# Rows scattered into expert slots while a sentence is routed, and experts' tiles loaded as contiguous rows

## The chip, the cores and the metric

The kernel runs on one core of a Trainium2 chip, in float32. The metric is the device time of one execution in microseconds (us); the time before is the median of three executions. Beside them stands one profiled execution with its trace, and every row shown below is from it. Engines: PE is TensorE, DVE is VectorE, ACT is ScalarE, POOL is GpSimd, SP is SyncE, which here only issues transfers.

## What is computed

```python
x = x + attention_a(layernorm(x))    # 8 sentences x 512 tokens x 256, 16 heads of 64, distance slopes, causal
x = x + experts(layernorm(x))
x = x + attention_b(layernorm(x))    # 8 heads of 128, rotary positions, causal
x = x + experts(layernorm(x))

def experts(x):                      # the same weights both times
    h = x * rsqrt(mean(x * x) + eps) * norm_w
    logits = h @ gate_w.T + gate_b
    vals, idx = top_k(logits, 2); wts = softmax(vals)          # 2 of 8 experts
    t1 = h @ mlp1_w[e].T + mlp1_b    # 256 -> 512
    act = min(glu, 7) * sigmoid(1.702 * glu) * (clip(lin, -7, 7) + 1)
    y = act @ mlp2_w[e].T + mlp2_b   # 256 -> 256
    return sum over the two chosen experts of y * wts
```

## The kernel before

Four stages follow each other: attention_a (0 to about 905 us), experts(0) (to 1186), attention_b (to about 1900), experts(1) (to 2195), and a tail that ends at 2215.5. Each engine has one instruction stream written out by hand, executed in order; engines meet through semaphores.

**Attention.** A unit u is a pair of heads; `bt, p = divmod(u, 8)` gives sentence bt (0 to 7) and unit p in it. A unit of attention_a takes 13.9 us, one of attention_b 11.4. In attention_a the POOL scales the probabilities of two heads per unit (`scale`, L1178) and adds some small normalising steps; in attention_b it does the rotary sums (L2058, L2069) and once a sentence a residual of 1024 columns (L2039).

**Routing.** Sentence bt-1 is routed during sentence bt. Its normalised rows are in the SBUF tile `hh`, one for all sentences; SP stores them to the DRAM tensor `hD` (`store`, 512 KB for each sentence and layer). The gate's top two give for each token two slots, a slot being expert * 4096 + rank among that expert's tokens. DVE writes them into `dI` (`route`, piece 4, L298; in attention_a in unit 6 of the sentence). POOL then scatters token numbers to those slots (`put_ids`, L311, an indirect DMA of 128 times 4 bytes to `slotD`, 8 for each sentence). As `dI` is one tile, L298 waits until the id scatters of the sentence before have landed (`d_sc`). SP fetches the id lists back (`fetch_ids`, L337), PE picks the used parts (`pick`), and DVE works out for each tile of 128 rows a column of `idx` (rows to gather) and of `place` (rows of the output) in six pieces (`places`).

**Experts.** Each experts stage has 71 tiles of 128 rows: 40 from the first six sentences, 31 from the rest. For a tile, POOL gathers 128 rows of 1 KB out of `hD` by `idx` (`gather`, L329); PE transposes them (L2286), multiplies up (L2301 to L2303), transposes the activation (L2312), multiplies down (L2325, L2327); ACT and DVE copy and activate between (ACT L2385, L2391, L2399, L2405, DVE L2473 to L2490); POOL scatters the 128 result rows to `yD` by `place` (`scatter`, L2600). Gathers run seven tiles ahead. The ids of the last two sentences are put inside the stage: eight before tile 0, mixed with the first gathers, and eight in tiles 16 to 27. The stream of POOL in the stage:

```python
for a in range(NS):
    if a + 7 < NS:
        gather(e, ph, q, a + 7)
    if 16 <= a < 28 and a % 3 != 0:
        put_ids(e, ph, BL, (a - 16) - (a - 16 + 1) // 3)
    ...
    scatter(a)
```

The functions that the change touches:

Of the kernel before, what the change touches and what calls it, by code (L numbers as in the profile page):

```python
# [59 lines left out]
def program(nc, T):  # L60
# [8 lines left out]
    with ctx:  # L69
# [4 lines left out]
        hD = [dram(f"hD{i}", [NT * 128, D]) for i in range(2)]  # L74
# [9 lines left out]
        hDv = [h.rearrange("(b p t) d -> b p t d", p=128, t=TT) for h in hD]  # L84
# [20 lines left out]
        idx = sb("idx", [128, NSP], I32)  # L105
        place = sb("place", [128, NSP], I32)
        etab = sb("etab", [1, NSP], I32)
# [23 lines left out]
        ls = sb("ls", [128, 2, L1])  # L131
        pl = sb("pl", [128, 2, L1])
# [140 lines left out]
        def route(e, q, ph, bt, piece, if8=None):  # L273
# [20 lines left out]
            else:  # L294
                e.wait_ge(r_op, 2 * s + 2)
                if s:
                    e.wait_ge(d_sc, 128 * s)
                e.scalar_tensor_tensor(dI[:], if8[:, :, 0:2], float(NT * 128), dF[:], ALU.mult, ALU.add).then_inc(r_sl, 1)  # L298
# [16 lines left out]

        Gs = []

        def gather(e, ph, q, a):
            if a == 0:
                e.wait_ge(r_ls, 4 * ph + 2)  # L320
                e.wait_ge(q.d_h, 16 * K1)
                e.wait_ge(q.p_xs, NB - 2)
            if a == L1:
                e.wait_ge(r_ls, 4 * ph + 4)
                e.wait_ge(q.d_h, 16 * NB)
# [27 lines left out]
        def listing(e, ph, k, piece):  # L353
# [61 lines left out]
            elif piece == 11:  # L415
                e.wait_ge(r_tab, b + 10 + k)
                if ph or k:
                    e.wait_ge(r_val, 2 * ph + k)
                e.tensor_scalar(Sel[:, 0, 0:n], ra[:, 0:n], cst[:, C_P:C_P + 1], None, ALU.is_equal)
# [30 lines left out]
        def places(e, ph, k, piece):  # L450
            n, off, b = (L1, L2)[k], (0, L1)[k], 4 * (2 * ph + k)
            v, w = ls[:, 0, 0:n], ls[:, 1, 0:n]
# [3 lines left out]
            elif piece == 1:  # L456
                e.wait_ge(r_st, b + 1)
                e.tensor_scalar(pl[:, 0, 0:n], v, float(NT * 128), float(NT * 128), ALU.is_gt, ALU.mult).then_inc(r_st, 1)
            elif piece == 2:
                e.scalar_tensor_tensor(pl[:, 1, 0:n], v, 0.0, cst[:, C_PAD + off:C_PAD + off + n], ALU.is_equal,  # L460
                                       ALU.mult).then_inc(r_st, 1)
            elif piece == 3:
                e.tensor_scalar(w, v, -1.0, 0.0, ALU.add, ALU.max).then_inc(r_st, 1)
            elif piece == 4:
                e.wait_ge(r_st, b + 4)
# [2376 lines left out]
```

## Time and profile before

| what | value |
|---|---|
| median of three executions | 2229.8 us (2229.5 to 2231.53) |
| profiled execution | 2217.43 us, span 2215.5 |
| PE busy | 2052.4 us, 93% |
| DVE, ACT busy | 1568.7 (71%), 1442.5 (65%) |
| POOL busy | 1308.6 (59%), 1466 instructions |
| mean granted PE clock | 0.98 |

A busy share counts time in which an engine has an instruction in work. "Idle before" is the time an engine sat before an instruction, with what released it; a releaser "remote" or "another core or an unknown queue" is one that the records of this core do not name, and "issue" is time in which no recorded thing was waited for.

### The profile page before, as it was taken

The page shows a single profiled execution, that of the slowest core. Times are in us where ns is not written, and L with a number is a line of the kernel's source. Part 1 is how long each engine was busy: PE and PEld are TensorE (multiplying, and loading weights), DVE is VectorE, ACT ScalarE, POOL GpSimd, SP SyncE. Part 2 cuts the span into 40 slices and gives each one's busy share as a digit, 9 for nine tenths or more (in the row PEclk, how much of TensorE's full clock was granted, in tenths as well). Part 3 has the DMA queues.
Part 4 walks back from the last instruction along what each step waited for, and adds up shares of the span by engine and source line. Part 5 has one row for each costly group of instructions (what it writes and reads, how often), then busy time and mean ns, then how long its engine had stood idle before and what let it go on. Part 6 is the DMA issues. An engine that isn't in the chain of part 4 may idle for free.

```text
span 2215.5 us, 38087 instructions
## 1 busy us (share of the span) xinstructions
PE 2052.4 (93%) x11638; PEld 1629.8 (74%) x11638; DVE 1568.7 (71%) x4433; ACT 1442.5 (65%) x3763; POOL 1308.6 (59%) x1466
## 2 busy tenths in 40 slices
PE   7899999999999999797998999999999999888895
PEld 6677777777777776575776787887878877676774
DVE  7867676868686868465666778677786776656567
ACT  5768787878686867433444868767777676633344
POOL 4665464646464655566665556667576565556563
PEclk9999999999999999999999999999999999999998
DMA  4330020101010000523341101011010001533347
GB/s 147 133 111 30 1 30 1 30 1 30 1 30 1 20 1 22 176 94 77 103 146 58 39 30 39 12 38 46 13 39 30 1 20 58 169 84 97 98 127 246
DMA packets 59932, 134.42 MB, mean 61 GB/s; under 512 B 12948, under 2 KB 31156, under 8 KB 58840
## 3 DMA queue, kind: packets, MB, share of 16 engines
q1 hardware_dynamic: 42008, 94.68, 12.8%
q0 software_dynamic: 17728, 37.32, 6.5%
q8 instruction: 100, 1.64, 0.4%
q14 instruction: 96, 0.79, 0.2%
HBM read 83.59 MB, written 48.40 MB: 60 GB/s over the span
## 4 chain that ended last, share of the span: by engine, by line
PE 68%; DVE 13%; ACT 6%; issue 5%; another core or an unknown queue 4%; POOL 1%; DMA 1%; SPq 0%; ACTq 0%; DVEq 0%; POOLq 0%
PE bank L639 5%; PE bank L657 5%; PE bank L2327 5%; PE bank L679 5%; PE bank L1568 4%; PE bank L624 3%; PE bank L625 3%; PE bank L1553 2%; PE bank L2301 2%; PE bank L2303 2%; PE bank L2302 2%; PE bank L1469 2%; PE bank L570 2%; PE bank L572 2%
## 5 line engine op out<-in xcount | busy, mean ns | idle before, releaser
L1178 POOL TENSOR_TENSOR P<-P,rc 128x128 f32<-128x128 f32 (+3 forms) x512 | 354.4, 723 | 342.0 <-DVE rc L984 341.8
L976 DVE CUSTOM_DVE_ANT_0 P<-bank,tab 128x512 f32<-128x512 f32 (+3 forms) x512 | 241.3, 485 | 105.6 <-PE bank L625 102.2
L807 ACT ACTIVATE P<-P,mn 128x128 f32<-128x128 f32 (+3 forms) x512 | 281.7, 552 | 34.2 <-DVE mn L976 30.7
L818 ACT COPY PT<-bank 128x512 f32<-128x512 f32 (+1 forms) x384 | 194.0, 516 | 107.3 <-PE bank L639 98.1
L2058 POOL TENSOR_TENSOR rf<-rp 128x512 f32<-128x512 f32 x128 | 163.9, 1281 | 134.9 <-DVE rp L1891 134.1
L2069 POOL TENSOR_TENSOR q<-rf,q 128x512 fp32r<-128x512 f32 x128 | 163.1, 1296 | 117.5 <-ACT q L1693 117.2
L639 PE MATMUL bank<-cst,P 128*128 128x128 f32 x1280 | 207.2, 276 | 15.4 <-POOL P L1178 9.6
L2600 POOL DMA_INDIRECT yD<-Yf,place x142 | 144.5, 1018 | 123.5 <-ACT Yf L2405 90.3
L624 PE MATMUL bank<-q 128*128 128x512 f32 (+3 forms) x512 | 185.2, 373 | 21.3 <-DVE mn L976 11.6
L329 POOL DMA_INDIRECT Gf<-hD,idx x142 | 144.8, 1020 | 74.4 <-issue 37.1
L639 PEld LDWEIGHTS bank<-cst,P 128*128 128x128 f32 x1280 | 153.0, 141 | 43.0 <-POOL P L1178 12.9
L952 DVE TENSOR_TENSOR q<-bank,q 64x512 fp32r<-64x512 f32 x256 | 175.8, 687 | 7.3 <-ACT q L798 1.3
L2399 ACT COPY ATf<-bank 128x256 f32<-128x256 f32 x142 | 53.4, 376 | 176.5 <-PE bank L2312 81.3
L798 ACT CAST q<-bank 64x512 fp32r<-64x512 f32 x256 | 146.5, 572 | 11.2 <-PE bank L572 8.0
L1720 ACT ACTIVATE P<-P,rc 128x128 f32<-128x128 f32 (+3 forms) x256 | 123.1, 552 | 46.6 <-DVE rc L1906 46.6
L2327 PE MATMUL bank<-W2f,ATf 128*128 x568 | 153.2, 394 | 0.0
L657 PE MATMUL bank<-PT,V 128*64 128x512 f32 (+3 forms) x1024 | 152.0, 439 | 1.3 <-ACT PT L818 1.3
L625 PE MATMUL bank<-q 128*128 128x512 f32 (+3 forms) x512 | 152.4, 323 | 0.0
L1568 PE MATMUL bank<-PT,V 128*128 128x512 f32 (+3 forms) x512 | 151.6, 439 | 0.9 <-ACT PT L1730 0.8
L311 POOL DMA_INDIRECT slotD<-cst,dI x128 | 128.7, 1005 | 39.8 <-issue 32.1
L1710 ACT ACTIVATE P<-P,mn 128x128 f32<-128x128 f32 (+3 forms) x256 | 141.0, 555 | 0.4 <-DVE mn L1898 0.4
L1730 ACT COPY PT<-bank 128x512 f32<-128x512 f32 (+1 forms) x192 | 93.5, 517 | 72.2 <-PE bank L1553 72.0
(272 smaller groups left out, 6037.2 us busy)
## 6 DMA issues: line engine op xcount, KB each, us to landing
hD<-hh SPq DMA_DIRECT2D x16, 512.0 KB
yg<-yD SPq DMA_DIRECT2D x14, 512.0 KB, 4.6
X<-in_x SPq DMA_DIRECT2D x8, 512.0 KB, 4.6
stage<-in_w SPq DMA_DIRECT2D x8, 512.0 KB, 3.7
w1hD<-W1A SPq DMA_DIRECT2D x8, 512.0 KB
w1lD<-stage SPq DMA_DIRECT2D x8, 512.0 KB
rD<-xn SPq DMA_DIRECT2D x8, 512.0 KB
W1lf<-w1lD SPq DMA_DIRECT2D x1, 4096.0 KB
```

The costliest lines, as they stand in the source:

```text
L624: e.matmul(o, QS[:, k, hl, ts], KS[:, k, hl, 0:w], start=True, stop=False)
L625: i = e.matmul(o, QS[:, k, hl, ts], KL[:, k, hl, 0:w], start=False, stop=True)
L639: i = e.transpose(o[:, at:at + 128], P[:, h % 3, OFF[t] + cc * 128:OFF[t] + cc * 128 + 128], ident)
L657: i = e.matmul(bank[6][64 * hl:64 * hl + 64, cc * 128:512], V[:, g % 2, cc, col:col + 64], PT[:, hl, PTO[cc]:PTO[cc] + w], start=cc == 0, ...
L807: i = e.activation(ps, ps, ACT.Exp, bias=mn[:, pb, t:t + 1], scale=-1.0, accum_out=rs[:, pb, t:t + 1])
L818: e.copy(PT[:, h % 2, PTO[cs[0]]:PTO[cs[0]] + w], bank[4 + n % 2][:, 0:w]).then_inc(q.a_pt, 1)
L952: e.tensor_tensor(L, bank[j][own, :], H.bitcast(F32), ALU.subtract).then_inc(v_q, 1)
L976: e.tensor_tensor_reduce(out=P[:, pb, OFF[t]:OFF[t] + w], in0=score(h, t), in1=tab[:, 512 - w:512], scale=-SLOPES[h % 16], scalar=3e38, op ...
L1178: i = e.tensor_tensor(ps, ps, rc[:, h % 3, t:t + 1].broadcast_to([128, w]), ALU.mult)
L1568: i = e.matmul(bank[6][:, cc * 128:512], V[:, g % 2, cc, col:col + 128], PT[:, PTO[cc]:PTO[cc] + w], start=cc == 0, stop=cc == TT - 1)
L2058: e.tensor_tensor(rf[:, j], rp[:, j, 0], rp[:, j, 1], ALU.add).then_inc(p_rf, 1)
L2327: i = e.matmul(o, AT[:, k, kc], W2[:, ex, kc].rearrange("p x n -> p (x n)"), start=False, stop=kc == 1)
```

## The change

`hD` becomes `hS`, 8 * 4096 rows for each layer: a region of 4 MB for each expert. Each normalised row is written to its two slots when its sentence is routed. In parts:

- SP's 16 stores of `hh` to `hD` are gone. In their place `put_rows`: 128 POOL indirect scatters (8 for each sentence and layer) of 128 rows of 1 KB from `hh` to `hS` by `dI`. The next sentence's `hh` and `dI` wait until they landed (`q.d_h` to 128 * bt).
- SP gets `fill`, 16 transfers DRAM to DRAM, one for each sentence and layer: a rotary table of 128 times 4 KB is written to each of the 8 regions (4 MB each time), so that slots nobody takes hold finite numbers. Two for each layer at its start, the others each after the fetch of the sentence's input.
- The 142 POOL gathers are gone. SP issues 142 `load`s in their place: the start row is read from `rtab` into a register (`value_load`), and 128 consecutive rows, 128 KB, are loaded. Load a waits until tile a - 4 was transposed; loads 0 to 3 are issued before the stage. `rtab` is one small DVE instruction in the listing.
- `places` has three pieces in place of six (no `idx`).
- `put_ids` moves. Attention_a: it was two each after units 7, 0, 1 and 2; now rows stand there (units 6, 7, 0, 1) and ids follow at units 2 to 5, two each; in the last sentence four ids each at units 2 and 3. Attention_b: rows two at unit 6, three each at units 7 and 0; ids two each at units 1 to 4, in the last sentence four each at units 1 and 2. Inside experts: sentence 6's ids one each in tiles 0 to 7, its last rows before the stage, and sentence 7's eight ids and eight rows in tiles 16 to 27, four for three tiles.
- In attention_b L298 moves from step 53 to step 47 of the sentence. `pick` moves from tile 31 to 33, `places` from 32, 33 to 34 to 36. SP's other transfers of an experts stage are interleaved with the loads.

```diff
+        def put_rows(e, q, ph, bt, n, hh):
+            s = NB * ph + bt
+            t, j = divmod(n, 2)
+            if n == 0:
+                e.wait_ge(r_sl, s + 1)
+                e.wait_ge(d_z, 32 + 16 * (s + 1))
+            e.indirect_dma_start(hS[ph], bass.IndirectOffsetOnAxis(ap=dI[:, t, j:j + 1], axis=0), hh[:, t],
+                                 None).then_inc(q.d_h, 16)
+
+
+        def fill(e, ph, s):
+            e.wait_ge(d_z, 32 + 16 * (NB * ph + s))
+            block = hS[ph].rearrange("(k s p r) d -> s p k (r d)", k=E, s=NB, p=128)[s]
+            src = T["tab"][1][:, 1:3].rearrange("p a b -> p (a b)").rearrange("p (a n) -> p a n", a=1)
+            e.dma_start(block, src.broadcast_to([128, E, 1024])).then_inc(d_z, 16)
...
-        def gather(e, ph, q, a):
+        def load(e, ph, q, a):
             if a == 0:
-                e.wait_ge(r_ls, 4 * ph + 2)
-                e.wait_ge(q.d_h, 16 * K1)
+                e.wait_ge(r_sel, 2 * ph + 1)
+                e.wait_ge(q.d_h, 128 * K1)
...
             if a > 3:
                 e.wait_ge(f_x, NS * ph + a - 3)
-            rows = hD[ph][0:K1 * N] if a < L1 else hD[ph]
-            e.indirect_dma_start(Gs[ph][:, a % 4], None, rows, bass.IndirectOffsetOnAxis(
-                ap=idx[:, a:a + 1], axis=0)).then_inc(d_g[a % 4], 16)
+            row = e.value_load(rtab[0:1, a:a + 1], min_val=0, max_val=E * 32 - 1)
+            rows = hS[ph].rearrange("(n p) d -> p n d", p=128)[:, bass.ds(row, 1)]
+            e.dma_start(Gs[ph][:, a % 4], rows.rearrange("p n d -> p (n d)")).then_inc(d_g[a % 4], 16)
...
@@ POOL, attention_a, after each unit
-                        if p == 7 and bt and bt + 1 < NB:
-                            for n in range(4 if bt == K1 else 2):
-                                put_ids(e, 0, bt - 1, n)
-                        if bt == K1 + 1 and p == 0:
-                            for n in range(4, 8):
+                        if bt and p > 5:
+                            for n in (2 * p - 12, 2 * p - 11):
+                                put_rows(e, q, 0, bt - 1, n, hh)
+                        elif bt > 1 and p < 2:
+                            for n in (2 * p + 4, 2 * p + 5):
+                                put_rows(e, q, 0, bt - 2, n, hh)
+                        elif bt == K1 + 1 and p < 4:
+                            for n in range(4 * p - 8, 4 * p - 4):
                                 put_ids(e, 0, bt - 2, n)
-                        elif 1 < bt <= K1 and p < 3:
-                            for n in (2 * p + 2, 2 * p + 3):
+                        elif 1 < bt <= K1 and p < 6:
+                            for n in (2 * p - 4, 2 * p - 3):
                                 put_ids(e, 0, bt - 2, n)
...
@@ POOL, experts
-                        if a + 7 < NS:
-                            gather(e, ph, q, a + 7)
-                        if 16 <= a < 28 and a % 3 != 0:
-                            put_ids(e, ph, BL, (a - 16) - (a - 16 + 1) // 3)
+                        if a < 8:
+                            put(BL - 1, a)
+                        elif 16 <= a < 28:
+                            for n in range(4 * (a - 16) // 3, 4 * (a - 15) // 3):
+                                put(BL, n)
```

## Rows read from the trace of the kernel before

**Rows 1.** The page: busy time, share of the span, instructions.

```profile
PE 2052.4 (93%) x11638; PEld 1629.8 (74%) x11638; DVE 1568.7 (71%) x4433; ACT 1442.5 (65%) x3763; POOL 1308.6 (59%) x1466
```

**Rows 2.** Busy time by stage: window, length, engines, granted clock, DMA share, GB/s.

```profile
110.00:905.00 795.00, 771.93 (x4707) 599.10 (x4707) 590.50 (x1854) 602.19 (x1589) 448.59 (x612) 1.00 0.10 30
905.00:1190.00 285.00, 245.19 (x1230) 193.35 (x1225) 168.97 (x458) 112.87 (x317) 172.83 (x179) 0.96 0.35 100
...
1890.00:2195.00 305.00, 263.77 (x1356) 208.70 (x1354) 190.16 (x521) 134.60 (x380) 180.19 (x175) 0.96 0.40 121
```

**Rows 3.** Groups of POOL: busy us, mean ns, idle before and releasers.

```profile
L329 POOL DMA_INDIRECT Gf<-hD,idx x142 | 144.8, 1020 | 74.4 <-issue 37.1 <-PE bank L2286 21.6 <-DVE place L468 15.2
L2600 POOL DMA_INDIRECT yD<-Yf,place x142 | 144.5, 1018 | 123.5 <-ACT Yf L2405 90.3 <-issue 33.2
L311 POOL DMA_INDIRECT slotD<-cst,dI x128 | 128.7, 1005 | 39.8 <-issue 32.1 <-DVE dI L298 6.3 <-PE bank L1537 1.2
```

**Rows 4.** Waits in 905 to 1190: us in total, times, longest.

```profile
ACT ATf L2399 <- remote: 33.0, 10, 5.3
```

**Rows 5.** Waits in 1890 to 2216.

```profile
ACT ATf L2399 <- remote: 42.2, 12, 7.2
```

**Rows 6.** Timeline of one stall in experts(0), all engines: start, us, instruction, idle before.

```profile
1042.85 0.39 PE L2303 MATMUL bank<-W1A,XTlf 128*128 x1
...
1044.78 0.42 DVE L2479 TENSOR_SCALAR glf<-bank 128x256 f32<-128x256 f32 x1 [3.45 <-remote]
...
1046.21 0.37 ACT L2399 COPY ATf<-bank 128x256 f32<-128x256 f32 x1 [5.33 <-remote]
...
1046.72 0.41 PE L2312 MATMUL bank<-cst,acf 128*128 128x128 f32 x2 [3.49 <-ACT ATf L2399]
```

**Rows 7.** Timeline of PE, first instruction of two tiles without a stall.

```profile
1053.14 0.38 PE L2286 MATMUL bank<-cst,Gf 128*128 128x128 f32 x2
...
1055.95 0.38 PE L2286 MATMUL bank<-cst,Gf 128*128 128x128 f32 x2
```

**Rows 8.** Waits in 2172 to 2196, after the last gather of experts(1).

```profile
ACT ATf L2399 <- remote: 2.5, 1, 2.5
```

**Rows 9.** Timeline of units 5 and 6 of sentence 2, attention_a.

```profile
339.44 0.91 POOL L1154 TENSOR_TENSOR X<-X,bout 128x256 f32<-128x256 f32 x1
342.91 2.76 POOL L1178 TENSOR_TENSOR P<-P,rc 128x128 f32<-128x128 f32 x4 [2.57 <-DVE rc L984]
...
344.04 0.66 DVE L298 SCALAR_TENSOR_TENSOR dI<-if,dF 128x8 int32<-128x8 f32 x1
...
344.93 1.41 DVE L952 TENSOR_TENSOR q<-bank,q 64x512 fp32r<-64x512 f32 x2
...
346.49 0.39 PE L624 MATMUL bank<-q 128*128 128x512 f32 x1
```

**Rows 10.** Timeline: last id scatter before a fetch of the lists, and the fetch.

```profile
827.08 0.95 POOL L311 DMA_INDIRECT slotD<-cst,dI  x1 [0.30 <-issue]
...
835.79 0.37 SPq L337 DMA_DIRECT2D idT<-slotD  x1
...
2050.77 0.97 POOL L311 DMA_INDIRECT slotD<-cst,dI  x1 [0.30 <-issue]
...
2054.36 0.37 SPq L337 DMA_DIRECT2D idT<-slotD  x1
```

**Rows 11.** Timeline of SP: the transfer that the fill follows in sentence 2.

```profile
327.93 0.42 SPq L1256 DMA_DIRECT2D X<-in_x  x1
```

**Rows 12.** Window as in rows 2: the busiest stretch of DMA.

```profile
890.00:905.00 15.00, 10.45 (x74) 7.09 (x73) 11.67 (x46) 11.85 (x36) 7.70 (x12) 1.00 0.94 400
```

**Rows 13.** Timeline of attention_b: residual of one sentence; unit 4 and L298 of the next.

```profile
1436.67 2.41 POOL L2039 TENSOR_TENSOR xl<-X,xl 128x1024 f32<-128x1024 f32 x1
...
1534.62 1.28 POOL L2058 TENSOR_TENSOR rf<-rp 128x512 f32<-128x512 f32 x1 [0.88 <-DVE rp L1891]
...
1561.59 1.11 DVE L298 SCALAR_TENSOR_TENSOR dI<-if,dF 128x8 int32<-128x8 f32 x1
```

More of the change, by code:

```diff
@@ L1297, in sync @@
                             fetch_x(bt + 2)
+                        if bt and bt + 1 < NB:
+                            fill(e, 0, bt + 1)
                         if bt == 0:
@@ L1314, in sync @@
                             e.dma_start(w1lD[0:1, :, 0:512], first[1]).then_inc(d_w1o, 16)
+                            fill(e, 0, 0)
+                            fill(e, 0, 1)
+                    for a in range(4):
+                        load(e, 0, q, a)
                     e.wait_ge(d_w1o, 32 * E + 48)
@@ L2095, in gpsimd @@
                             residual(bt - 1)
-                        if u == NU - 1:
-                            for a in range(4):
-                                gather(e, 1, q, a)
                         if p == 7 and bt + 2 < NB:
@@ L2664, in sync @@
                         store_r(BL - 1)
+                        for a in range(4):
+                            load(e, ph, q, a)
                         e.wait_ge(q.a_q, 2 * NU)
@@ new lines, in sync @@
+                    for a in range(4, NS):
+                        load(e, ph, q, a)
+                        if a == 16:
+                            store_r(BL)
+                        if a == 37:
+                            fetch_ids(e, ph, 1)
+                        if not last:
+                            if a == 19:
+                                e.wait_ge(q.m_lg, 2 * NB)
+                                stage_in(0)
+                                stage_in(1)
+                            elif a % 4 == 0 and 28 <= a <= 64:
+                                stage_in((a - 20) // 4)
+                            if a == 64:
+                                begin[4](e)
+                            elif a == 65:
+                                begin[5](e)
+                        else:
+                            if a in (19, 22, 25, 28):
+                                fetch_r((a - 19) // 3)
+                            elif a in (45, 49, 53, 57):
+                                fetch_r((a - 29) // 4)
+                            if a == 65:
+                                for k in range(4):
+                                    e.wait_ge(d_y[k], 16 * ph * ((NS + 3 - k) // 4) + 16 * ((LA + 3 - k) // 4))
+                                e.wait_ge(q.h_in, NB)
+                                fetch_rows(0, 1)
+                                fetch_rows(0, 0)
+                            elif 65 < a < NS - 1:
+                                fetch_rows((a - 64) // 2, 1 - a % 2)
@@ L2765, in _ @@
             late = first[4](e)
-            second[4](e, late)
+            second[4](e, late, begin)
             late = third[4](e)
```

190 lines of the change are left out of this document (86 added, 104 removed).

## Prediction

> **What bounds the kernel now.** I read the page first: PE is busy 93% of the span, POOL 59% [rows 1]. Then the windows by stage: in attention_a PE works 771.93 us of 795 at full clock, so little is to be had there; in the first experts stage it works 245.19 of 285 us at a clock of 0.96, in the second 263.77 of 305 [rows 2]. The two stages hold 81 us in which PE idles, attention_a 23 us in 795. So the question is what the change does to PE's idle time in the experts stages, and whether what it puts into the attention stages breaks a cover there.
>
> A tile of an experts stage without a stall takes PE 1055.95 - 1053.14 = 2.81 us [rows 7]; 71 tiles would take 200 us, and the stage takes 285 with its start. What fills the gap is seen in the waits: ACT sits 33.0 us in 10 pieces before the copy of the transposed activation with a releaser the records don't name, up to 5.3 us each; in the second stage 42.2 us in 12 [rows 4, 5]. In one such stall, PE has begun the last up product at 1042.85 and is done within half a us; DVE takes the result up at 1044.78 and ACT at 1046.21, after 3.45 and 5.33 us of idle time, and PE then waits 3.49 us for ACT [rows 6]. Nobody was busy: engines are told late that PE is done. After the last gather of the second stage such waits are down to one of 2.5 us [rows 8], though the result rows are still scattered. The attention window 110 to 905 has no such row among its 25 longest waits, with its id scatters in groups of two to four. I read from this that the late signals come with dense indirect transfers of POOL, above all where gathers and scatters alternate without a gap.
>
> An indirect transfer holds POOL for 1.0 us and leaves 37.1 / 122 = 0.30 us before the next can start, 1.3 us together, whichever of the three kinds it is [rows 3]. A tile with gather and scatter costs POOL 2.6 us of PE's 2.81; one with an id scatter too costs 3.9.
>
> **The change part by part, experts.** It removes one indirect of each tile and adds no work to PE. POOL is at 1.3 us for most tiles, 2.6 in tiles 0 to 7, and 1.3 * (1 + 4/3) = 3.0 in tiles 16 to 27.
> - Late signals: 33.0 + 42.2 = 75.2 us of ACT's idle time [rows 4, 5]. PE loses less than ACT, 3.49 of 5.33 [rows 6], a factor of 0.65: 49 us. Bounds: 0 if they have nothing to do with the gathers, and 75 if PE loses all that ACT loses. I take 49: the part after the last gather [rows 8] speaks for nearly all.
> - Tiles 16 to 27: POOL's mean is (2 * 3.9 + 2.6) / 3 = 3.5 us before and 3.0 after, against PE's 2.81, so 12 * 0.5 = 6 us for each stage; about half lies under the stalls already counted, so 3 each, 6 in all (0 to 12).
> - Loads: 128 KB for each tile of 2.81 us is 47 GB/s, the DMA engines have moved 400 in a busy stretch [rows 12], and a load is issued three tiles (8.4 us) before its use. Its cover is these 8.4 us. I take 0. The wait of SP for `f_x` holds the transfers queued behind it on SP; those are input rows and weights with tiles of slack, 0 to 5 us.
> - The four gathers before the stage waited for `place`, 15.2 us [rows 3], but PE is still busy with the last output projection then. I take 0 (0 to -4, as a free POOL could bring tile 4 sooner).
> Sum for experts: -49 - 6 = -55 us, bounds +5 and -91 (75 + 12 + 4).
>
> **Attention_a, the id scatters moved later.** This is where I see a new wait. Before, the ids of sentence bt-2 were put by unit 2. Now their last pair stands after unit 5: POOL ends L1154 at 339.44 + 0.91 = 340.35, so the second scatter starts at about 341.8 [rows 9]. L298 of the next sentence comes on DVE at 344.04 [rows 9], and waits for them to land. How long a landing takes is bounded by the fetches of the lists, which wait for it: 2054.36 - 2050.77 = 3.6 us and 835.79 - 827.08 = 8.7 us, both with the fetch's own issue in them [rows 10]. Landing is thus at 345.4 to 350.5; I take a little over the middle, 348.3 (6.5 us), as this is an attention stage, like the 8.7. DVE stands 4.3 us. Queued behind L298 are the maxima of the next scores and at 344.93 the rotation of q, 1.41 us, for which PE's scores at 346.49 wait with 346.49 - 346.34 = 0.15 us of slack [rows 9]. PE loses about 4 us in each of sentences 2 to 6: +20 us. Bounds: 1.4 - 0.15 = 1.2 and 6.3 a sentence, +6 to +32.
> The fill bears on this. It starts right after the fetch at 327.93 [rows 11] and moves 4 MB. At 400 GB/s [rows 12] that is 10.5 us, over by 339, before the ids. At half that speed it is 21 us and lies across them.
> The Trainium skill, "DMA: Bandwidth & Descriptors", section "Latency and other measured facts", says that copies between HBM tensors whose rows lie 4 MiB apart ran at about half the rate of closer or padded rows (103 against 214 GB/s). The fill writes pieces 4 MB apart; by that figure a fill would last about 40 us. No row of before has such a transfer.
>
> **Attention_a, POOL.** The 64 row scatters come on top of the ids, and each pair of either costs 2.6 us. POOL works 448.59 of 795 us [rows 2] and otherwise waits for DVE before a scale; that idle time is the cover. After unit 5, where it has L1154 to do as well, 2.57 us are left before the next scale against a pair's 2.6 [rows 9]; if such a cover is gone, PE's transposes of the scaled probabilities are late by what is missing. Only the groups of four of the last sentence don't fit (5.2 us). +3 us (0 to 6).
>
> **Attention_b, POOL.** Here POOL is tighter: rotary sums follow the residual L2039, 2.41 us [rows 13], without a pause. The id pair now put behind it pushes PE's scores; half of 2.6 us is caught by later slack, 1.25 * 5 sentences = 6, and +3 for the groups of four in the last sentence: +9 (0 to 20). L298 is moved six steps of 11.4 / 7 = 1.6 us earlier, from 1561.59 to about 1552; the ids after unit 4 are issued behind the rotary sum of 1534.62, so by 1538.5 [rows 13], and with 8.7 us to land they are 5 us early: 0. Stores of `hh` removed, DVE pieces removed: off the path, 0.
>
> **Sum.** 2217.4 - 55 + 20 + 3 + 9 = 2194 for a profiled execution, 23 us less. The runs shown have a median 12 us over the profiled one; I carry the difference: 2229.8 - 23 = 2207.
>
> **Rivals.**
> 1. *The late signals stay.* They are not tied to gathers; an SP load or any dense traffic also brings them. For it: in the experts stages much besides the gathers is going on, and the DMA share is 0.35 to 0.40 against 0.10 [rows 2]. Against: rows 8, where traffic goes on. Then only the 6 us of tiles 16 to 27 and some 4 more remain: -10 + 32 = +22, 2252. This is the case on the other side: it decides once less than 26 us of the 49 go.
> 2. *The fill holds the ids.* At 21 to 40 us a fill lies across the ids put at 340 to 343; if their landing is 9 us later, PE loses 45 us more in the five sentences: -23 + 45 = +22, again 2252; at 4 us later, 2227.
> The Trainium skill, same page, section "Queues, rings and completion order", says that a completion's semaphore write comes after all earlier writes of that DMA engine, across its queues. By this rule the ids of a busy fill are signalled only with the fill's issued pieces; no row here shows it.
> 3. *Landing is quick* (3.6 us), PE loses more than 0.65 of ACT's idle time, and attention_b takes less: -62 + 6 + 3 + 5 = -48, 2182.
>
> **How the numbers follow.** Forecast 0.52 (own range 2192 to 2222); rival 1 0.2; rival 2 0.16, of which a third ends near 2227 and the rest slower; rival 3 0.12. Within 0.2%, about 4.5 us and what this kernel's measurement can tell, lies 0.07 in all. Faster: 0.50 + 0.12 + 0.01 = 0.63. Slower: 0.30. The range goes from 2182 to 2252.
>
> **What would show it.** Right: the rows with the unnamed releaser in both experts stages fall under 10 us, tiles follow at about 2.9 us, each stage is some 27 us shorter; in attention_a a wait of DVE for L298 on the ids, 4 us in each of five sentences, and that stage 20 us longer; attention_b 9 us longer. Wrong: stages of 285 us with the same ACT waits (rival 1), or waits of DVE over 8 us in sentences 2 to 6 with DMA busy (rival 2), or PE waiting for a load.

## The result, and the profile after

The changed kernel takes 2277.65 us (median of four executions, 2273.32 to 2281.53), the kernel before beside it 2230.06 (2229.5 to 2231.53). The ratio is 1.0212, with a 95% interval of 1.0192 to 1.0232: 2.1% slower. The profiled execution has a span of 2279.7 us against 2215.5, so 64.2 us more; the medians differ by 47.6, because the profiled execution of before lies 12 us under its median and that of after 4 us over its own. What follows explains the 64.2. The page of the changed kernel, where [rows 1] stood before:

```profile
span 2279.7 us, 38939 instructions
...
PE 2068.0 (91%) x11638; PEld 1647.5 (72%) x11638; DVE 1585.4 (70%) x4425; ACT 1443.7 (63%) x3763; POOL 1293.3 (57%) x1452
...
PEclk9999998989899999999999999999999999989998
```

POOL is a little less busy, PE works the same instructions. (PEclk is the granted clock of PE in 40 equal slices, in tenths of full speed.) A cut by stage shows where the time went. A stage is read here from the first and last transposition of the experts' tiles, which are the group L2286 before and L2301 after (first and last start are the last numbers of a row). Before, experts(0) and then experts(1):

```profile
L2286 PE MATMUL bank<-cst,Gf x142: 272/273/421, 913.7 to 1173.0; 128*128 128x128 f32 x142
...
L2286 PE MATMUL bank<-cst,Gf x142: 272/273/421, 1931.5 to 2183.2; 128*128 128x128 f32 x142
```

After:

```profile
L2301 PE MATMUL bank<-cst,Gf x142: 270/273/421, 993.0 to 1229.6; 128*128 128x128 f32 x142
...
L2301 PE MATMUL bank<-cst,Gf x142: 271/273/421, 2009.4 to 2245.3; 128*128 128x128 f32 x142
```

| stretch | before | after | change | forecast |
|---|---|---|---|---|
| start to the first tile (attention_a) | 913.7 | 993.0 | +79.3 | +23 |
| first to last tile, experts(0) | 259.3 | 236.6 | -22.7 | -27.5 |
| to the first tile of experts(1) (attention_b) | 758.5 | 779.8 | +21.3 | +9 |
| first to last tile, experts(1) | 251.7 | 235.9 | -15.8 | -27.5 |
| to the end | 32.3 | 34.4 | +2.1 | 0 |

The waits of the whole changed kernel hold the row that explains most of the first line:

```profile
DVE dI L298 <- issue: 65.4, 5, 19.2
```

Five times DVE stood before L298, once in each of sentences 2 to 6, 65.4 us together, up to 19.2. Sentence 2, the longest, where [rows 9] showed the same place before, on DVE:

```profile
343.77 0.09 DVE L988 DVE_READ_ACCUMULATOR2_ANT mn<- 128x1 f32 x1
363.00 0.17 DVE L298 SCALAR_TENSOR_TENSOR dI<-if,dF 128x8 int32<-128x8 f32 x1 [19.15 <-issue]
363.09 0.28 DVE L988 CUSTOM_DVE_ANT_0 P<-bank,tab 128x128 f32<-128x128 f32 x1
```

and on POOL, the id scatters that it waits for:

```profile
341.56 0.96 POOL L311 DMA_INDIRECT slotD<-cst,dI  x1 [0.30 <-issue]
342.66 2.75 POOL L1190 TENSOR_TENSOR P<-P,rc 128x128 f32<-128x128 f32 x4
```

The last scatter starts at 341.56 and DVE goes on at 363.00: 21.4 us. In the other four sentences the same distance is 15.8, 13.3, 13.8 and 12.4 us, so 15.3 on average. The trace calls the releaser "issue": it names none. L298 waits for the semaphores of the id and row scatters, and the ids are the last of them; the run with early ids below shows that it is they. What PE stood for in sentence 2:

```profile
346.22 0.39 PE L636 MATMUL bank<-q 128*128 128x512 f32 x1
...
363.43 0.69 PE L636 MATMUL bank<-q 128*128 128x384 f32 x1 [16.16 <-DVE mn L988]
```

The first scores were not held; the next ones waited for a maximum of DVE, which is queued behind L298. All such waits of PE together are 60.5 us in this trace, the longest 16.2.

The windows of that stretch have PE's busy time first, then PEld, DVE, ACT, POOL, and at the end clock, DMA share and GB/s:

```profile
325.00:335.00 10.00, 9.51 (x73) 7.16 (x73) 8.85 (x31) 7.96 (x23) 7.54 (x8) 1.00 0.77 214
335.00:345.00 10.00, 9.15 (x63) 6.76 (x62) 7.71 (x28) 7.42 (x19) 7.94 (x11) 1.00 1.15 112
345.00:355.00 10.00, 2.27 (x13) 1.67 (x11) 0.00 (x0) 0.00 (x0) 0.41 (x1) 0.79 0.81 101
355.00:363.00 8.00, 0.00 (x0) 0.00 (x0) 0.00 (x0) 0.00 (x0) 0.00 (x0) 0.50 0.49 78
```

The fill, issued at 327.8, goes on past the end of the stall at about 100 GB/s, not at the 400 of [rows 12]. It is slow before the last two scatters start at 340.25 and 341.56: between 335 and 340 it already moves 80, and the pair before them started at 327.97 and 329.28, just behind the fill.

```profile
329.28 0.96 POOL L311 DMA_INDIRECT slotD<-cst,dI  x1 [0.30 <-issue]
```

```profile
335.00:340.00 5.00, 4.15 (x30) 2.69 (x30) 4.75 (x15) 4.20 (x14) 3.54 (x5) 1.00 1.38 80
```

PE stands with DVE, and its granted clock falls to 0.50, the level of 1.2 GHz, while it stands; the stall costs a little more than its own length, since the window 365 to 385 still shows 0.84. Of the 79.3 us, 65.4 are these waits of DVE; the other 14 are a remainder, put down to the clock and to POOL (5 us of it, as the run with early ids shows).

In the experts stages the waits of ACT with an unnamed releaser, before the copy of the transposed activation (`ATf`), did shrink. They are called late signals below. Experts(0), where [rows 4] stood, and experts(1), where [rows 5] stood:

```profile
ACT ATf L2414 <- remote: 21.7, 7, 5.9
```

```profile
ACT ATf L2414 <- remote: 9.7, 3, 3.8
```

75.2 us became 31.4.

### The profile page after: what moved, and what is told of

Read it like the earlier page. It is cut to its first block, busy times and chain, and to the rows that moved or that the text cites. A ratio compares the mean times of both kernels' runs of the same rounds, so it can differ in the third digit from the quotient of the medians.

```text
span 2279.7 us, 38939 instructions
## 1 busy us (share of the span) xinstructions
PE 2068.0 (91%) x11638; PEld 1647.5 (72%) x11638; DVE 1585.4 (70%) x4425; ACT 1443.7 (63%) x3763; POOL 1293.3 (57%) x1452
## 4 chain that ended last, share of the span: by engine, by line
PE 69%; DVE 14%; issue 8%; POOL 3%; ACT 3%; DMA 2%; SPq 1%; another core or an unknown queue 1%; DVEq 0%; POOLq 0%; ACTq 0%
PE bank L691 5%; PE bank L2342 5%; PE bank L1586 5%; PE bank L669 4%; PE bank L651 4%; PE bank L636 3%; PE bank L2316 3%; PE bank L2318 3%; PE bank L2317 3%; PE bank L637 3%; PE bank L1571 2%; PE bank L1487 2%; PE bank L1488 2%; PE bank L1489 2%; PE bank L582 2%
## 5 line engine op out<-in xcount | busy, mean ns | idle before, releaser
L819 ACT ACTIVATE P<-P,mn 128x128 f32<-128x128 f32 (+3 forms) x512 | 281.8, 553 | 96.8 <-DVE mn L988 93.0
L2622 POOL DMA_INDIRECT yD<-Yf,place x142 | 144.1, 1015 | 248.7 <-ACT Yf L2420 240.3
L651 PE MATMUL bank<-cst,P 128*128 128x128 f32 x1280 | 211.5, 281 | 16.6 <-POOL P L1190 11.4
L636 PEld LDWEIGHTS bank<-q 128*128 128x128 f32 x512 | 98.7, 193 | 102.5 <-DVE mn L988 79.3
L810 ACT CAST q<-bank 64x512 fp32r<-64x512 f32 x256 | 147.0, 574 | 11.4 <-PE bank L584 8.3
L322 POOL DMA_INDIRECT hS<-hh,dI x128 | 128.9, 1007 | 41.6 <-issue 32.3
```

The costliest lines, as they stand in the source:

```text
L636: e.matmul(o, QS[:, k, hl, ts], KS[:, k, hl, 0:w], start=True, stop=False)
L651: i = e.transpose(o[:, at:at + 128], P[:, h % 3, OFF[t] + cc * 128:OFF[t] + cc * 128 + 128], ident)
L819: i = e.activation(ps, ps, ACT.Exp, bias=mn[:, pb, t:t + 1], scale=-1.0, accum_out=rs[:, pb, t:t + 1])
```

## The experiments

All ran beside the kernel before on the same chip, and the ratio is always to it. The runs came in five groups; in four of them the kernel before took 2143 to 2148 us, in one 2222, and in the result above 2230. Compare times only inside a group. Attention_a, and with 3 us more attention_b, take the same in every trace of the kernel before (913.7 to 916.0, and 755.6 to 758.5), so these stages are compared across groups too; the experts stages are not. Stages are cut as above, each from one profiled execution.

| run | group: before | median | ratio (95%) | attention_a | experts(0) | attention_b | experts(1) |
|---|---|---|---|---|---|---|---|
| four fills | 2144.4 | 2193.5 | 1.0224 (1.0207 to 1.0241) | 954.0 | 217.2 | 771.1 | 223.5 |
| fill by expert | 2144.4 | 2231.7 | 1.0395 (1.0375 to 1.0416) | 984.5 | 215.4 | 775.6 | 225.2 |
| fill late | 2144.4 | 2219.6 | 1.0353 (1.0332 to 1.0373) | 944.4 | 217.1 | 801.1 | 220.3 |
| before + fills | 2144.4 | 2144.8 | 0.9998 (0.9989 to 1.0008) | 917.3 | 220.1 | 755.7 | 217.2 |
| changed kernel again | 2142.9 | 2238.6 | 1.0442 (1.0408 to 1.0477) | 986.5 | 215.8 | 776.1 | 223.1 |
| ids early | 2142.9 | 2167.9 | 1.0121 (1.0087 to 1.0154) | 921.4 | 215.6 | 776.8 | 216.8 |
| ids early, cast 1 step earlier | 2142.9 | 2173.3 | 1.0137 (1.0103 to 1.0170) | 924.4 | 216.1 | 774.9 | 224.0 |
| the same, second scatter | 2142.9 | 2196.9 | 1.0249 (1.0220 to 1.0279) | 920.5 | 233.8 | 775.7 | 235.1 |
| ids early, cast 2 steps earlier | 2147.2 | 2213.1 | 1.0309 (1.0292 to 1.0325) | 924.9 | 216.6 | 819.6 | 225.1 |
| the same, ids 3, 3, 0, 2 | 2147.2 | 2198.3 | 1.0238 (1.0220 to 1.0256) | 924.0 | 218.1 | 804.6 | 216.1 |
| kernel before, trace | 2147.2 | 2146.2 | - | 916.0 | 221.0 | 755.6 | 217.2 |
| ids early, reduction | 2221.8 | 2204.6 | 0.9933 (0.9908 to 0.9959) | 925.0 | 231.9 | 775.9 | 234.8 |
| ids early, 3, 3, 2 in b | 2221.8 | 2202.2 | 0.9912 (0.9888 to 0.9936) | 924.9 | 228.4 | 781.3 | 234.6 |
| ids early, 4, 4 in b | 2221.8 | 2207.6 | 0.9922 (0.9897 to 0.9948) | 926.8 | 229.6 | 777.3 | 240.3 |
| reduction and 3, 3, 2 | 2221.8 | 2204.6 | 0.9929 (0.9904 to 0.9953) | 925.5 | 226.6 | 779.1 | 238.1 |
| 3, 3, 2 again | 2148.0 | 2171.0 | 1.0107 (1.0087 to 1.0128) | 923.3 | 216.8 | 770.9 | 223.2 |
| the same, second scatter | 2148.0 | 2197.0 | 1.0226 (1.0208 to 1.0243) | 919.9 | 231.8 | 768.7 | 240.3 |
| kernel before, third trace | 2148.0 | 2146.6 | - | 915.2 | 222.2 | 756.4 | 217.4 |

**Is it the fill?** Half the fills, none in sentences 2 to 6. The run leaves out slot blocks 3 to 6 of each expert, which this input does not reach. The edit in attention_a; it does the same in attention_b:

```diff
-                        if bt and bt + 1 < NB:
+                        if bt == 1:
                             fill(e, 0, bt + 1)
```

> The changed kernel with 4 fills a layer in place of 8 (slot blocks 0, 1, 7 at the start, 2 in sentence 1), so that no fill runs in sentences 2 to 6. This leaves out the fill of slot blocks 3 to 6 of each expert, which this input does not reach. Theory F (a fill of some 40 us holds up the landing of the ids, and L298 waits for it): the five waits of DVE at L298, 65.4 us in all, fall to 2 to 5 us each, attention_a loses about 50 us, the time falls to about 2215 to 2225. Rival P (the ids are late by their place alone, after unit 5, whatever else the DMA engines do): the waits stay above 10 us and the time stays above 2265.

Attention_a fell from 986.5 (the changed kernel in a like group) to 954.0. The waits before L298 fell too, from 65.4 in the result and 51.7 in that like group to 27.5, 5.5 each, just above the 2 to 5 each that I expected:

```profile
DVE dI L298 <- issue: 27.5, 5, 9.1
```

In sentence 2, the longest again, DVE goes on at 354.56, with the last id scatter started at 343.14 and the DMA engines idle in both windows:

```profile
354.56 0.17 DVE L298 SCALAR_TENSOR_TENSOR dI<-if,dF 128x8 int32<-128x8 f32 x1 [9.13 <-issue]
```

```profile
335.00:345.00 10.00, 9.16 (x66) 6.82 (x64) 8.80 (x29) 8.47 (x23) 6.38 (x9) 1.00 0.00 0
345.00:355.00 10.00, 3.86 (x21) 3.00 (x19) 0.84 (x6) 0.57 (x3) 1.99 (x3) 0.89 0.00 0
```

So 128 numbers of 4 bytes alone take 11.4 us to land here, and 7.9, 8.6, 5.2 and 5.7 in the other four sentences, 7.8 on average. The same kernel with its fills, in the like group, takes 12.8, 15.4, 12.8, 12.1 and 10.1, 12.6 on average:

```profile
DVE dI L298 <- issue: 51.7, 5, 13.1
```

In its sentence 2 the fill is as slow (115 GB/s in the window 335 to 345), yet the ids land after 12.8 us, when the fill is still going on; so the 21.4 us of the result are the largest of ten, and not the rule. Late ids without a fill cost 33 us of attention_a (954.0 against the 921.4 of the run with early ids below), and the fill doubles that (986.5).

**Is the fill slow by its 4 MB pitch?** That is the distance between its consecutive 4 KB pieces. The same bytes as eight contiguous transfers:

```diff
-            block = hS[ph].rearrange("(k s p r) d -> s p k (r d)", k=E, s=NB, p=128)[s]
...
-            e.dma_start(block, src.broadcast_to([128, E, 1024])).then_inc(d_z, 16)
+            block = hS[ph].rearrange("(k s p r) d -> k s p (r d)", k=E, s=NB, p=128)
+            for k in range(E):
+                e.dma_start(block[k, s], src).then_inc(d_z, 16)
```

> The changed kernel with each fill issued as 8 transfers of 512 KB, one for each expert, each to one contiguous stretch, in place of one transfer whose consecutive 4 KB pieces lie 4 MB apart. Bytes and places are the same. If the pitch makes the fill slow (theory F with the pitch as its reason), a fill lasts 20 us or less, is over by 348, and the waits at L298 fall to about 5 us: 2220 to 2235. If transfers from DRAM to DRAM are slow as such, a fill still lasts about 40 us and the time stays within 5 us of 2278.

Attention_a is 984.5 against 986.5, and the waits at L298 are 55.1 against 51.7: the pitch is not the reason. And a fill is not slow as such either, as the kernel before with fills shows below.

**Fill after L298.** The edit in attention_a; the same wait is added in attention_b:

```diff
                         if bt and bt + 1 < NB:
+                            e.wait_ge(r_sl, bt)
                             fill(e, 0, bt + 1)
```

> The changed kernel with each fill of sentences 1 to 6 held back until L298 of that sentence is done. Theory F: the ids land with idle DMA engines and the waits at L298 fall to about 4 us each, 2225 to 2240, unless the row scatters, which now meet the fill, are late for the next use of hh (then a wait shows at L947, up to 5 us a sentence). Rival P: no change, above 2265.

The waits at L298 are nearly as without a fill (22.7 against 27.5), the first of these two rows is new:

```profile
ACT yg L1785 <- DMA yg<-yD: 43.6, 5, 11.2
...
DVE dI L298 <- issue: 22.7, 5, 6.1
```

Attention_a falls to 944.4, but attention_b rises to 801.1: the fill now runs when the rows `yg` are fetched, and ACT waits for them 43.6 us in five pieces.

**The fill alone, in the kernel before.** Its ids are out before the fill starts. `zS` is a pair of tensors nobody reads:

```diff
+                        if bt and bt + 1 < NB:
+                            fill(e, 0, bt + 1)
```

> The kernel before with the 16 fills added at the same places, into two tensors nobody reads. Its ids are put by unit 2, before the fill starts. Theory F with the late ids as the second half of the cause: within 5 us of before, as nothing waits for a transfer during a fill. If a fill costs by itself (fetches of inputs late, memory traffic), it is slower by 10 to 60 us.

No change, 0.9998. The window of the fill in sentence 2:

```profile
335.00:345.00 10.00, 9.45 (x64) 6.97 (x63) 8.90 (x30) 8.89 (x25) 4.02 (x7) 1.00 1.03 305
```

With the same 4 MB pitch the fill moves 305 GB/s and is over by 350. In the changed kernel the same window had 112. So the two slow each other: the fill that meets four id scatters is issued at 327.8 and still moving at 363, this one is issued at 330.3 and over by 349; and the ids land 5 us later on average. With row scatters of 1 KB a row it is otherwise: in the run with the late fill two of them start at 355.25 and 356.57, and the fill moves 219 and 158 GB/s in the next 4 us and 330 after that. The small writes of the ids are thus the likelier reason, but no run changed their size alone.

**The changed kernel again, and ids early.** The first because the kernel before was 4% faster in this group than beside the result:

> The changed kernel itself, once more, since the kernel before took 2144 us on the chip of the first experiments and 2230 on that of the result. Theory G (removing the gathers removes late signals, which only some chips have): on a chip where the kernel before takes about 2144 us, its experts stages have nothing to gain, and the changed kernel is slower by about 95 us (4.4%); on a chip where before takes about 2230, by about 48 (2.1%). Rival (the late signals are noise of single runs): 2.1% on every chip.

1.0442, as theory G forecast for such a group. But the record names the same chip for the group with 2143 and the one with 2222 us, which speaks against the theory's words that only some chips have late signals. The second run moves id scatters earlier, with them two row scatters of each sentence from unit 1 to unit 0, and leaves the fill:

```diff
-                        elif bt > 1 and p < 2:
-                            for n in (2 * p + 4, 2 * p + 5):
-                                put_rows(e, q, 0, bt - 2, n, hh)
-                        elif bt == K1 + 1 and p < 4:
-                            for n in range(4 * p - 8, 4 * p - 4):
-                                put_ids(e, 0, bt - 2, n)
-                        elif 1 < bt <= K1 and p < 6:
-                            for n in (2 * p - 4, 2 * p - 3):
-                                put_ids(e, 0, bt - 2, n)
+                        elif bt > 1 and p < 4:
+                            if p == 0:
+                                for n in range(4, 8):
+                                    put_rows(e, q, 0, bt - 2, n, hh)
+                            for n in ((0, 1, 2), (3, 4), (5, 6), (7,))[p]:
+                                put_ids(e, 0, bt - 2, n)
```

> The changed kernel with the id scatters of attention_a put earlier: rows of a sentence at units 6, 7 (two each) and 0 (four), ids at units 0 to 3 (three, two, two, one). The fill stays as and where it is. Theory F (the loss in attention_a needs ids under way when L298 comes; the fill alone is harmless): no wait at L298, attention_a within 8 us of the kernel before, about 75 us less than the changed kernel. Rival (the fill slows attention_a in other ways): less than 40 us of it comes back.

Attention_a takes 921.4 in place of 986.5, 5 us above the kernel before; no wait at L298 is left. The fill's window:

```profile
335.00:345.00 10.00, 9.45 (x61) 6.83 (x60) 8.88 (x29) 8.78 (x25) 4.57 (x6) 1.00 1.02 324
```

324 GB/s. The place of the eight 4-byte scatters of each sentence was worth 65 us.

**Attention_b: a cast of 7 us.** In four sentences a cast of DVE that took 0.30 us before takes 7.23. From the run with early ids, DVE and then POOL beside it:

```profile
1414.93 7.23 DVE L228 CAST if<-i 128x32 f32<-128x32 uint32 x1
```

```profile
1411.78 0.98 POOL L311 DMA_INDIRECT slotD<-cst,dI  x1 [0.17 <-issue]
1413.07 0.96 POOL L311 DMA_INDIRECT slotD<-cst,dI  x1 [0.30 <-issue]
1414.05 2.55 POOL L2084 TENSOR_TENSOR q<-rf,q 128x512 fp32r<-128x512 f32 x2
1416.55 5.56 POOL L2066 TENSOR_TENSOR X<-X,yg 128x256 f32<-128x256 f32 x8
```

The cast ends at 1422.16, POOL's row of ten tensor operations at 1422.11. I tried to move it away.

```diff
-                            elif at == 39:
+                            elif at == 38:
```

> As the run with early ids, and in attention_b the top-two pieces of DVE with the cast L228 stand one step (1.6 us) earlier. Theory H: in four sentences of attention_b this cast of 128 x 32 numbers takes 7.2 us in place of 0.3, because it meets a run of POOL tensor operations without a pause (L2087, then eight of L2069), and it is held until they end. One step earlier it comes before them: 0.3 us again, attention_b about 3 us a sentence shorter, 12 in all. Rival (the cast is long for another reason): it stays at 7.2 us.

> As the run with early ids, and the pieces of DVE with the cast L228 stand two steps earlier in attention_b (step 37 in place of 39). One step was too little: the cast then came at 1418.62, still behind the first of POOL's ten tensor operations in a row (1417.75 to 1425.83), and ended with the last. Theory H: two steps earlier it meets POOL's two id scatters instead and takes 0.3 us; attention_b is about 3 us shorter in each of four sentences, 12 in all. Rival (the cast waits for POOL's indirect transfers too, or for something else): still 7.2 us, or about 2.

One step earlier it came at 1418.62 and took 7.25 us; two steps earlier it came at 1425.94 behind a POOL row that began at 1425.91, took 7.92, and attention_b rose by 43 us, to 819.6. The next run adds ids three, three, none and two:

> As the run before, and in attention_b the id scatters of sentences 2 to 6 stand three, three, none and two after units 1, 2, 3 and 4, in place of two each: none behind the residual L2057 in unit 3. Theory: the remaining loss of about 1 us a sentence before PE's scores after unit 3 goes, 5 us in all. Rival: the third scatter after units 1 and 2 costs as much there, no change.

The cast fell to 1.1 us in three of the four sentences and took 8.0 in the fourth, and attention_b stayed 49 us longer than before (804.6). All three are misses. My reading is that DVE's pieces, moved earlier, stand before more urgent ones; no run separates that from the cast. Then the cast was replaced, back at step 39, by an instruction of another kind with the same result:

```diff
-                e.tensor_copy(if8[:], i8[:]).then_inc(q.v_top, 1)
+                e.reduce_sum(if8.rearrange("p t k -> p (t k)"), i8.rearrange("p t (k a) -> p (t k) a", a=1), AX).then_inc(q.v_top, 1)
```

> As the run with early ids (cast back at step 39), but the whole numbers of the top two are turned into floats by a DVE reduction over an axis of one element instead of a copy that casts. Theory H (DVE's copy and POOL's tensor operations exclude each other, and the copy is let through only when POOL's row of them ends): the reduction takes 0.2 to 0.4 us where the cast took 7.2, and attention_b is 2 to 3 us shorter in each of four sentences, some 10 us in all. Rival (DVE is slow there because POOL's traffic slows whatever reads SBUF): the reduction takes 7 us too.

```profile
L228 DVE TENSOR_REDUCE if<-i x16: 177/184/186, 221.4 to 2007.8; 128x32 f32<-128x32 uint32 x16
```

All sixteen take 0.18 us; the one at 1531.21 begins within a POOL row that runs from 1530.33 to 1538.4. That the cast is held by POOL's row and the reduction is not is thus shown, and its price is shown to be about nothing: attention_b is 775.9 against 776.8, and 779.1 against 781.3 with and without the reduction inside this group. The forecast of 10 us less was a miss. The residuals L2054 of two sentences, with the reduction:

```profile
1518.06 2.40 POOL L2054 TENSOR_TENSOR xl<-X,xl 128x1024 f32<-128x1024 f32 x1
...
1612.93 2.40 POOL L2054 TENSOR_TENSOR xl<-X,xl 128x1024 f32<-128x1024 f32 x1
```

94.9 us a sentence, where the kernel before has 90.9. What remained was POOL:

```diff
-                            for n in (2 * p - 2, 2 * p - 1):
+                            for n in ((0, 1, 2), (3, 4, 5), (6, 7), ())[p - 1]:
                                 put_ids(e, 1, bt - 2, n)
```

> As the run with early ids, cast unchanged; in attention_b the ids of sentences 2 to 6 stand three, three and two after units 1, 2 and 3 and none after unit 4, so that POOL's ten tensor operations are not pushed towards the cast from unit 4. Theory H: the cast meets them as in the kernel before (0.3 us) if POOL is back in time after unit 3, and attention_b is some 10 us shorter. Rival: POOL is still late from units 1 to 3 and the cast stays at 7.2 us.

> As the run before with the ids four and four after units 1 and 2, none after 3 and 4. Theory H: cast 0.3 us, as POOL has two units to catch up; groups of four cost PE 1 to 2 us there, so attention_b is 5 to 10 us shorter than with two after each. Rival: the four cost more than the cast (2.9 us a sentence).

> The run with the reduction and the run with three, three and two ids together. If both theories hold, attention_b is within 5 us of the kernel before's 743 us, and the whole within 0.5% of it on a chip without late signals.

> The run with ids three, three and two in attention_b once more. In a group of runs where the kernel before takes about 2144 us: attention_b about 748 us in place of the 764 of the run with early ids, and the whole between 0.3% and 0.8% slower than before. In a group where it takes 2220 or more: again 0.7 to 1.1% faster than before.

With no ids after unit 4 the cast takes 0.3 us again and the residuals follow at 91.5 us (the run again):

```profile
1506.64 2.40 POOL L2054 TENSOR_TENSOR xl<-X,xl 128x1024 f32<-128x1024 f32 x1
...
1598.15 2.40 POOL L2054 TENSOR_TENSOR xl<-X,xl 128x1024 f32<-128x1024 f32 x1
```

So it is the pair after unit 4, not the cast, that costs 3.4 us a sentence; the cast is short in both runs. The stage is still 15 us longer than before, 770.9, and 9 of that are one stall in sentence 2, where the residual follows after 100.6 us, when SP issues a fetch and the fill just as two id scatters go out at 1408.61 and 1409.90:

```profile
1410.00:1420.00 10.00, 2.23 (x3) 1.18 (x4) 2.62 (x7) 3.24 (x9) 2.55 (x3) 0.60 1.25 34
```

DVE waits 10.6 us there with an unnamed releaser, the DMA engines are full (a share of 1.25) and move 34 GB/s. This run missed its forecast (1.0107 where 1.003 to 1.008 was expected) by about this stall. The first run with three, three and two (attention_b 781.3, no shorter than with early ids alone, where 10 us less was forecast) holds a PE stall of 10.5 us at the same place. Four and four is no better than three, three, two, and the two remedies together no better than one: the medians of these four runs lie within 6 us. The forecast for the two together missed for attention_b (779.1, 24 us above before, where 5 were allowed).

**The late signals.** A trace of the kernel before in a group where it takes 2147 us:

> The kernel before itself, for its trace on the chip of these experiments. Theory G: on a chip where it takes about 2144 us, its experts stages show no waits with an unnamed releaser and last 228 to 233 us each, not the 272 and 263 of the trace shown before; attention_a and attention_b last the same as there, within 5 us.

Its experts stages take 221.0 and 217.2 us, not 259.3 and 251.7, with the same gathers, and no ATf wait has an unnamed releaser. Against 215.8 and 223.1 of the changed kernel, there is nothing to gain. The two stages together thus lost, by an estimate across groups, 73 us to late signals in the result's kernel before (511.0 against 438.2) and 34 in the changed kernel (472.5 against 438.9); so PE lost about all that ACT lost before `ATf`, 75.2 and 31.4, and the 39 us between them are the whole gain of the experts stages. The group with 2222 us fits: the kernel before is some 75 us slower there than in the groups without late signals, and the version with ids three, three and two 31. Does POOL's density bring the late signals? A second scatter was put before each result scatter, once for each base:

```diff
                         e.wait_ge(a_y, T0 + a + 1)
+                        e.indirect_dma_start(zD[ph], bass.IndirectOffsetOnAxis(ap=place[:, a:a + 1], axis=0), cst[:, 0:D],
+                                             None).then_inc(d_y[a % 4], 16)
```

> As the run with early ids and the earlier cast, and in the experts stages each result scatter is preceded by a second indirect scatter of constants, by the same places, into a tensor nobody reads: POOL again has two indirect transfers for each tile. It computes what the reference computes. Theory G on a chip with late signals: the waits with an unnamed releaser come back to 60 us or more and the stages are 15 to 20 us longer each; on a chip without them, within 5 us of the run without the second scatter, as POOL's 2.6 us for each tile lie under PE's 2.8.

> The same with a second indirect scatter of constants, into a tensor nobody reads, before each result scatter of the experts stages: POOL again has two indirect transfers a tile. It computes what the reference computes. Theory G, in a group of runs with late signals: waits with an unnamed releaser before ATf rise from about 14 to over 28 us in each experts stage. In a group without: none, and about 17 us a stage more than without the second scatter, as in the earlier run. Rival (late signals have nothing to do with POOL's transfers): the same waits with and without.

> The kernel before, for its trace in the same group of runs: with late signals its ATf waits with an unnamed releaser are 30 us or more in each experts stage, else none.

Both runs of it fell into groups where the kernel before took 2143 and 2148 us. No unnamed releaser came in the experts stages; the stages grew by 11 to 18 us, where the first had been expected within 5. The waits of experts(0) of the second point at the result tile Yf, which is free only when its scatter has landed, now behind another (7.7 us without the second scatter):

```profile
ACT Yf L2418 <- DMA yD<-Yf,place: 30.0, 14, 6.2
```

The third trace of the kernel before was again one without late signals. In the one group where the kernel before took 2222 us only versions without gathers have a trace:

```profile
ACT ATf L2411 <- remote: 13.5, 4, 4.7
```

That is experts(0) of the run with the reduction. Versions without gathers lose less than half as much in both groups that have late signals; but whether the gathers bring the late signals, or only suffer from them, stays open, and so does why some groups have none.

## Why the prediction was wrong

The forecast was 2207 and faster; the result is 2277.65, outside the range.

- **The step that failed** is the landing of the ids in attention_a: "At 400 GB/s [rows 12] that is 10.5 us, over by 339, before the ids", and a landing of 6.5 us, together +20. Measured are landings of 12.4 to 21.4 us, 15.3 on average, waits of 65.4 in five sentences, and +79 for the stage. Rival 2 is what happened, the fill holds the ids, and nearly in its size: 13.1 us of wait a sentence in place of 4.3, where it said 9 more. The fill was sized by a transfer that met no scatter. Even alone it moves 305 to 324 GB/s and takes about 18 us (330.3 to 348), which puts its end, issued at 327.8, at an estimated 346, not out of the way of ids put at 340; beside ids it falls to about 100, and each slows the other. The landing alone was the smaller part: 5.2 to 11.4 us, 7.8 on average, where 6.5 had been taken between bounds of 3.6 and 8.7.
- The mechanism behind it was right in the main: L298 waits, and DVE's next pieces are queued behind it. But PE did not stand for the rotation of q and its 0.15 us of slack; it stood for the maxima, which the prediction names as queued too. Each microsecond of wait cost the stage a little more than one (65 us for 51.7 of waits, in the like group); the sum had no term for PE's granted clock, which falls to 0.50 in the stall and is not back in the window after it. The early ids took back 65 of the 70 us.
- Rival 2 gave 2252. That the result lies above is the experts stages, 16 us short of their gain, and attention_b, 12 us dearer. The 12 us between the profiled execution and the median, carried over from before, did not hold either.
- **Experts, -55.** Measured -38.5, in the right direction: the unnamed waits before `ATf` fell from 75.2 to 31.4, by 43.8, where the forecast let them go altogether. The factor 0.65 was too small: by the groups without late signals PE lost 73 us for ACT's 75.2. The 6 us of tiles 16 to 27 are not seen: in the groups where the kernel before takes 2143 to 2148 us both kernels take 438 to 439 us for the two stages (221.0 + 217.2 and 215.8 + 223.1). So two errors partly cancelled. "The part after the last gather speaks for nearly all" claimed too much. A profile of one execution can't tell a loss of the kernel from one of the moment.
- **Attention_b, +9.** Measured +21.3, mis-sized. POOL is the cause, as said, but the costly pair is the one after unit 4, which the prediction put at 0 because the ids land in time. PE's waits for DVE's maxima fall from 22.2 us in the stage with that pair (early ids) to 11.4 without it (three, three and two again); that they come by way of POOL's delayed row is argued, not shown.
- **Attention_a, POOL, +3.** About right: 5 us remain with early ids.
- **Loads, 0.** Right: no PE wait for a load is among the larger ones.
- The two rules of the Trainium skill, "DMA: Bandwidth & Descriptors". The section "Latency and other measured facts" has copies with rows 4 MiB apart at 103 GB/s; this case's traces show 305 and 324 GB/s in the windows of a fill whose pieces lie 4 MB apart, and about 100 only beside id scatters, where eight contiguous transfers cost the stage the same (984.5 us against 986.5). The measurement decides: here the pitch did not matter, and nothing ties the 100 GB/s beside the scatters to it. The section "Queues, rings and completion order" has completions written after all earlier writes of an engine; that the landing of ids stretched from 7.8 to 12.6 us on average beside a fill agrees with it, but no run here separates it from plain queueing.
- The Trainium skill, "SBUF — State Buffer", section "Who interferes with whom", says that a DVE cast can contend with GpSimd for a shared pair of ports, and that whoever comes first has it for its whole instruction while the other is blocked. The trace agrees in kind; but the cast stood for the rest of a row of ten POOL instructions, 7.2 to 8.0 us, not for one of them. A reduction was never held (0.18 us in each of the 16).

No version beats the kernel before everywhere. With ids early in attention_a and three, three and two in attention_b the change is 0.9% faster than before (0.9912, interval 0.9888 to 0.9936) in the one group with late signals that has it, and 1.1% slower (1.0107, 1.0087 to 1.0128) in one without.

## What to carry to other kernels

When a transfer is moved, look for who waits for its landing, and size the landing under the traffic that the same change adds; a few 4-byte scatters next to a large fill took 10 to 21 us to land, and moving the last of them two units earlier was worth 65 over five sentences. A queue that has slack on average may have none behind one instruction: try the place, not the sum. And before counting on a loss that a trace names no releaser for, look at a second execution at another time.

## What was not expected of the hardware

- An indirect scatter of 128 numbers of 4 bytes, the second of a pair, landed 5.2 to 11.4 us after its start without a fill (the longest with idle DMA engines, 343.14 to 354.56), and 10.1 to 21.4 us beside a fill.
- The windows of a fill show 305 to 324 GB/s when it is alone and about 100 with such scatters around it. In one window of 10 us the DMA engines were full and moved 34 GB/s, and DVE and ACT stood 10.6 and 9.5 us for a releaser that the trace does not name.
- A DVE cast of 128 x 32 numbers took 7.2 to 8.0 us when it began within a row of ten POOL tensor operations, and ended with the row; as a reduction, 0.18.
- The same kernel took 2143 to 2148 us in four groups of runs, 2222 and 2230 in two others; between 2146 and 2230 the difference is in its experts stages (438 against 511 us); 2222 has no trace. The record names the same chip for the groups with 2143 and 2222.
